# Two adaptive-norm blocks on one core: a new order at the end of the first layer, its last dense rows read from PSUM, and the second layer's first weights loaded and split inside it

## What is computed

```
mod = silu(c) @ wmod                       # per layer: sa, ca, ga, sb, cb, gb
# first layer
h = layernorm(x) * (1 + ca) + sa
x = x + ga * small_attention(h)
h = layernorm(x) * (1 + cb) + sb
p = softmax(h @ centroids.T / 0.1)         # 64 clusters
query_sel = any(p > 0.01, over clusters)   # per row
cluster_sel = any(p > 0.01, over all rows) # per cluster
dense = h @ weight.T + bias
x = x + gb * where(query_sel & cluster_sel[assignments], dense, 0)
# second layer
h = layernorm(x) * (1 + ca) + sa
q, k, v = h @ w_q, h @ w_k, h @ w_v        # 32 heads on 8 key heads, width 128
x = x + ga * causal_attention(q, k, v) @ w_o
h = layernorm(x) * (1 + cb) + sb
x = x + gb * (silu(h @ gate) * (h @ up)) @ down
```

## Time and profile before

| | us |
|---|---|
| median of 3 runs | 1952.21 (1950.08 to 1952.51) |
| the profiled execution | 1954.34 |
| its span, first to last instruction | 1952.6 |
| TensorE busy | 1858.4 (95%) |
| VectorE busy | 1229.1 (63%) |
| ScalarE busy | 1127.5 (58%) |
| GpSimd busy | 468.3 (24%) |

### The profile page before, as it was taken

The page is one execution under the profiler, slowest core; times in us unless marked ns, Lnnn a source line. Parts: engine busy times, 40 slices in busy tenths (PEclk is TensorE's granted clock), DMA queues, the critical chain, the costliest instruction groups (busy, mean ns, idle before and its releaser), DMA issues. The chain is left out here.

```text
span 1952.6 us, 30013 instructions
## 1 busy us (share of the span) xinstructions
PE 1858.4 (95%) x9227; PEld 1548.6 (79%) x9227; DVE 1229.1 (63%) x2962; ACT 1127.5 (58%) x2617; POOL 468.3 (24%) x474
## 2 busy tenths in 40 slices
PE   6897489999999999999999999999999979999999
PEld 4465378888888888888888888888888867788887
DVE  5577566766666666666666666667666676543534
ACT  5463466666666666666666666656666654433423
POOL 3121441414233231313423121240312052010010
PEclk8798699999999999999999999999999999999999
DMA  9100265565646545466654645455554475211010
GB/s 353 64 1 1 108 180 161 167 185 156 201 138 195 157 152 172 144 199 184 200 173 148 178 131 175 132 164 153 155 175 121 151 221 168 70 55 56 14 59 21
DMA packets 170381, 275.30 MB, mean 141 GB/s; under 512 B 18745, under 2 KB 111929, under 8 KB 170305
## 3 DMA queue, kind: packets, MB, share of 16 engines
q1 hardware_dynamic: 167760, 270.18, 44.9%
q10 hardware_dynamic: 2544, 4.19, 0.7%
HBM read 173.65 MB, written 100.66 MB: 140 GB/s over the span
## 5 line engine op out<-in xcount | busy, mean ns | idle before, releaser
L2018 DVE CUSTOM_DVE_ANT_0 ps<-ps,mask 128x512 f32<-128x512 f32 (+3 forms) x512 | 236.3, 524 | 339.7 <-PE ps L1573 339.7
L1534 PE MATMUL ps<-hA,wq 128*128 128x512 f32 x1536 | 386.0, 400 | 1.1 <-DVE qT L2003 0.8
L1606 PE MATMUL ps<-wo,oT 128*128 128x512 f32 x1536 | 372.1, 393 | 5.6 <-POOL wo L1392 5.6
L1842 ACT ACTIVATE pt<-pd 128x1280 fp32r<-128x1280 f32 x128 | 163.2, 1275 | 353.8 <-PE ps L1588 344.2
L1606 PEld LDWEIGHTS ps<-wo,oT 128*128 128x128 f32 x1536 | 286.7, 189 | 64.3 <-POOL wo L1392 5.8
L1534 PEld LDWEIGHTS ps<-hA,wq 128*128 128x128 f32 x1536 | 279.0, 188 | 57.9 <-issue 0.9
L1823 ACT ACTIVATE probs<-ps,nmax 128x512 f32<-128x512 f32 (+3 forms) x512 | 262.7, 532 | 47.4 <-DVE nmax L2018 47.3
L1831 ACT ACTIVATE probs<-probs,rinv 128x512 f32<-128x512 f32 (+3 forms) x512 | 246.2, 552 | 31.5 <-DVE rinv L2024 31.5
L1588 PE MATMUL ps<-pt,V 128*128 128x512 f32 (+2 forms) x1152 | 251.8, 348 | 8.1 <-DVE pt L2042 8.1
L1573 PE MATMUL ps<-kT,qT 128*128 128x512 f32 (+2 forms) x1152 | 224.9, 340 | 0.0
L1588 PEld LDWEIGHTS ps<-pt,V 128*128 128x128 f32 x1152 | 196.2, 189 | 34.7 <-issue 10.2
(11 more groups left out here) (214 smaller groups left out, 2554.9 us busy)
## 6 DMA issues: line engine op xcount, KB each, us to landing
turned_blocks<-tp SPq DMA_DIRECT2D x128, 640.0 KB, 2.9
pd<-turned_blocks SPq DMA_DIRECT2D x512, 160.0 KB, 3.3
wq_in<-in_L_attn_w_q_dram SPq DMA_DIRECT2D x16, 1024.0 KB, 6.4
wo_in<-in_L_attn_w_o_dram SPq DMA_DIRECT2D x16, 1024.0 KB, 7.0
wm<-in_L_wmod_dram SPq DMA_DIRECT2D x6, 2048.0 KB, 13.3
X<-in_L_attn_x_dram SPq DMA_DIRECT2D x4, 1024.0 KB, 11.2
wk_in<-in_L_attn_w_k_dram SPq DMA_DIRECT2D x16, 256.0 KB, 3.8
wv_in<-in_L_attn_w_v_dram SPq DMA_DIRECT2D x16, 256.0 KB, 4.1
```

Source lines behind the costliest of these rows:

```text
L1534: last = nc.tensor.matmul(ps[:, bank, :], w[i][:, c, cols], hT[k][:, c, b * S:(b + 1) * S], start=(c == 0 and n == 0), stop=(c == DC - 1 a ...
L1606: last = nc.tensor.matmul(ps[:, bank, :], oT[x_][:, b, h, r * P:(r + 1) * P], wo[y_][:, h, :], start=(h == 0 and n == 0), stop=(h == GQ - ...
L1842: nc.scalar.activation(flat(pt[0][:]), flat(pd[:, u % 2]), ACT.Copy).then_inc(phi_done, 1)
L2018: nc.vector.tensor_tensor_reduce(out=v, in0=v, in1=mask[:, TB * P - KEYS[i]:], scale=-1.0, scalar=3e38, op0=ALU.add, op1=ALU.min, accum_ou ...
```

## The change

- DVE: `with_dense` becomes two functions, `gate_dense` (L747) and `add_rows` (L751). The gate of sequence 0 stands before `add_outputs(2)`, its adds between the two halves of `add_outputs(3)`. cluster_hits(2), gate and adds of sequence 1 stand before the second layer's modulations; the gate of sequence 2 stands between `cluster_logits(3)` and `cluster_hits(3)`, its adds behind the threshold. Gate and adds of sequence 3 come after the first two sequences have been selected and their statistics taken. `inverse_2(0)` stands in the middle of select_rows(1), `inverse_2(1)` between gate and adds of sequence 3.
- The last sequence's dense tiles (12 to 15) aren't drained: the gate reads them from PSUM. Tiles 14 and 15 use the banks of the attention update (BANK_U), and `turn(3, ...)` uses banks 0 and 1 alone.
- PE: linear(14) stands before the transpose of the maximum.
- ACT: the four last drains are gone, `modulated_2(0)` stands before root_2(1), and modulated_2 waits for `mods_done`.
- SP: the load of the first Q weights goes to a tile over X's first tiles (`wq_next`). It is issued in the first block, once X's first four tiles are stored and normal_2(0) has read them, and the stores of tiles 4 to 15 are queued behind it.
- Pool: the first K and V weights are split in the first block, into memory over `dense`, once sequence 0 is selected. The prologue of the second block begins with the wait for the Q load and the first Q head.

The semaphore `w_hi` of the second block is renamed `w_high` and made earlier; this and its uses are left out below.

```diff
@@ -222,7 +222,13 @@
         l0 = ExitStack()
         with l0:
+            with ExitStack() as early:
+                wq_next = sb(early, "wq_next", [P, DC, D], F32)
             X = sb(l0, "X", [P, NT, D], F32)
+            with ExitStack() as early:
+                wk = [sb(early, f"wk{i}", [P, DC, HD], F32R) for i in range(2)]
+                wv = [sb(early, f"wv{i}", [P, DC, HD], F32R) for i in range(2)]
             with ExitStack() as early:
                 c_in = sb(early, "c_in", [B, 2, D], F32)
@@ -329,7 +337,11 @@
             def bank_of(k):
                 if k < DC:
                     return (0, 1, BANK_U, BANK_U + 1)[k]
-                return k % 2 + (BANK_U if k >= DC * (len(JOBS) - 2) else 0)
+                return k % 2
+            def bank_of_dense(t):
+                return BANK_D + t % 2 if t < NT - 2 else BANK_U + t % 2
             def tiles_of(b):
                 return slice(TB * b, TB * (b + 1))
@@ -372,6 +384,11 @@
                     for t in range(NT):
                         sp.wait_ge(x2_done, t + 1)
                         sp.dma_start(mid_t[t // TB][:, t % TB, :], X[:, t, :]).then_inc(mid_stored, 16)
+                        if t == TB - 1:
+                            sp.wait_ge(mid_stored, 16 * TB)
+                            sp.wait_ge(xh_2, 1)
+                            sp.dma_start(wq_next[:], w_q.rearrange("(c p) n -> p c n", p=P)[:, :, 0:D]).then_inc(q_in, 16)
                     sp.wait_ge(mid_stored, 16 * NT)
                     sp.wait_ge(kv_in, 32)
@@ -420,6 +437,15 @@
                             pool.wait_ge(taken, chunk(2, b, c) + 1)
                             nc.gpsimd.tensor_tensor(hP[b % 2][:, 1, c, :], hT2[:, c, :], hP[b % 2][:, 0, c, :].bitcast(F32),
                                                     ALU.subtract).then_inc(low2, 1)
+                    pool.wait_ge(x2_done, TB)
+                    pool.wait_ge(kv_in, 32)
+                    nc.gpsimd.tensor_copy(wk[0][:], wk_in[:]).then_inc(w_high, 1)
+                    pool.wait_ge(w_high, 1)
+                    nc.gpsimd.tensor_tensor(wk[1][:], wk_in[:], wk[0][:].bitcast(F32), ALU.subtract).then_inc(wk_split, 1)
+                    nc.gpsimd.tensor_copy(wv[0][:], wv_in[:]).then_inc(w_high, 1)
+                    pool.wait_ge(w_high, 2)
+                    nc.gpsimd.tensor_tensor(wv[1][:], wv_in[:], wv[0][:].bitcast(F32), ALU.subtract).then_inc(wv_split, 1)
                     for i in range(PAIR):
                         for c in range(DC):
                             pool.wait_ge(taken, chunk(3, i, c) + 1)
@@ -617,10 +643,7 @@
                     modulated2(3, range(2, DC))
                     drain(11)
                     copy_columns2(3)
-                    drain(12)
                     clusters(3)
-                    for t in range(TB * (B - 1) + 1, NT):
-                        drain(t)
                     def root_2(i):
                         act.wait_ge(var_2, i + 1)
@@ -634,6 +657,7 @@
                         last.then_inc(xh_2, 1)
                     def modulated_2(i):
+                        act.wait_ge(mods_done, 4)
                         for c in range(DC):
                             k = chunk(3, i, c)
                             act.wait_ge(turned, k + 1)
@@ -642,8 +666,8 @@
                     root_2(0)
                     normal_2(0)
+                    modulated_2(0)
                     root_2(1)
-                    modulated_2(0)
                     normal_2(1)
                     modulated_2(1)
@@ -713,8 +737,9 @@
                         by_tile = lambda k: red[:, k].rearrange("p (t e) -> p t e", t=TB)
                         nc.vector.tensor_tensor(o_t[:, :, 0:E0], by_tile(2), by_tile(1), ALU.mult).then_inc(o_done, 1)
-                    def add_outputs(b):
-                        for t in range(TB * b, TB * (b + 1)):
+                    def add_outputs(b, tiles=range(TB)):
+                        for r in tiles:
+                            t = TB * b + r
                             dve.wait_ge(upd_ps, t + 1)
                             nc.vector.tensor_tensor(X[:, t, :], X[:, t, :], ps[:, BANK_U + t % 2, :], ALU.add).then_inc(x1_done, 1)
@@ -739,14 +764,21 @@
                         link(nc.vector.tensor_scalar(qsel[:, tiles_of(b)], cred[:, 2], THRESHOLD, None, ALU.is_gt))
                         link(nc.vector.tensor_tensor(top[:], pr[:] if b == 0 else top[:], pr[:], ALU.max))
-                    def with_dense(b):
+                    def gate_dense(b):
                         dve.wait_ge(rows_sb, 2 * B)
                         for t in range(TB * b, TB * (b + 1)):
-                            dve.wait_ge(drained, t + 1)
-                            last = nc.vector.scalar_tensor_tensor(dense[:, t, :], dense[:, t, :], qsel[:, t:t + 1], gb_rows[:, b, :],
+                            if b < B - 1:
+                                dve.wait_ge(drained, t + 1)
+                                rows = dense[:, t, :]
+                            else:
+                                dve.wait_ge(dense_ps, t + 1)
+                                rows = ps[:, bank_of_dense(t), :]
+                            last = nc.vector.scalar_tensor_tensor(dense[:, t, :], rows, qsel[:, t:t + 1], gb_rows[:, b, :],
                                                                   ALU.mult, ALU.mult)
                         link(last)
+                    def add_rows(b):
                         for t in range(TB * b, TB * (b + 1)):
                             last = nc.vector.tensor_tensor(dense[:, t, :], dense[:, t, :], X[:, t, :], ALU.add)
                         link(last)
@@ -803,6 +835,7 @@
                     cluster_logits(0)
                     outputs(2)
                     cluster_hits(0)
+                    gate_dense(0)
                     add_outputs(2)
                     statistics2(2)
@@ -811,31 +844,34 @@
                     cluster_logits(1)
                     outputs(3)
                     cluster_hits(1)
-                    add_outputs(3)
+                    add_outputs(3, range(2))
+                    add_rows(0)
+                    add_outputs(3, range(2, TB))
                     statistics2(3)
                     cluster_logits(2)
                     normal2(3)
+                    cluster_hits(2)
+                    gate_dense(1)
+                    add_rows(1)
                     dve.wait_ge(mods_sb, len(MODS))
                     mods_finish(link, 1, MOD_SA, 6, tmp_g)
                     dve.sem_inc(mods_done, 1)
-                    cluster_hits(2)
-                    with_dense(0)
-                    with_dense(1)
                     cluster_logits(3)
-                    with_dense(2)
+                    gate_dense(2)
                     cluster_hits(3)
                     nc.vector.tensor_reduce(topc[:], top[:].rearrange("p t k -> p k t"), AX.X, ALU.max).then_inc(chosen, 1)
                     dve.wait_ge(chosen, TOP_TURNED)
                     link(nc.vector.tensor_reduce(topv[:, 0:1], ps[0:NCL, BANK_M, 0:P], AX.X, ALU.max))
                     link(nc.vector.tensor_scalar(topv[:, 1:2], topv[:, 0:1], THRESHOLD, None, ALU.is_gt))
                     nc.vector.tensor_scalar(selb[:], ones[:], topv[:, 1:2], None, ALU.mult).then_inc(chosen, 1)
-                    with_dense(3)
+                    add_rows(2)
                     dve.wait_ge(chosen, ROWS_SPREAD)
-                    def select_rows(b):
-                        for t in range(TB * b, TB * (b + 1)):
+                    def select_rows(b, tiles=range(TB)):
+                        for r in tiles:
+                            t = TB * b + r
                             nc.vector.copy_predicated(X[:, t, :], ps[:, BANK_P, :].bitcast(I32), dense[:, t, :]).then_inc(x2_done, 1)
-                        dve.wait_ge(x2_done, TB * (b + 1))
+                        dve.wait_ge(x2_done, t + 1)
                     def inverse_2(i):
                         v = tiles_of(i)
@@ -846,11 +882,14 @@
                     select_rows(0)
                     statistics(mv_2, 0, TB, var_2)
-                    select_rows(1)
+                    select_rows(1, range(2))
                     inverse_2(0)
+                    select_rows(1, range(2, TB))
                     statistics(mv_2, TB, 2 * TB, var_2)
+                    gate_dense(3)
+                    inverse_2(1)
+                    add_rows(3)
                     select_rows(2)
-                    inverse_2(1)
                     select_rows(3)
                     statistics(mv_2, 2 * TB, NT, var_2)
@@ -943,11 +982,13 @@
                     def linear(t):
                         b, r = t // TB, t % TB
-                        if t >= 2:
+                        if 2 <= t < NT - 2:
                             pe.wait_ge(drained, t - 1)
+                        if t >= NT - 2:
+                            pe.wait_ge(x1_done, NT)
                         if r == 0:
```

(17 more changed lines are left out.)

13 lines of the change are left out of this document (7 added, 6 removed).

## The result

The changed kernel took 1942.06 us, median of five runs (1936.46 to 1942.76), against 1952.21 for the kernel before beside it (also five runs, 1950.08 to 1958.59): ratio 0.9932, 95% interval 0.9914 to 0.9951. (The quotient of the two medians is 0.9948.) Its profiled execution took 1936.46 us, span 1934.7. In two later sessions, each beside fresh runs of the kernel before, the same program gave 1936.73 against 1956.03 (0.990, 0.9878 to 0.9921) and 1937.53 against 1954.41 (0.9921, 0.9906 to 0.9936). Over all four sessions the kernel before has a median of 1954.75 in 66 runs, over three of them the changed one 1937.99 in 17, with a standard deviation of 2.8 to 2.9 us each. The medians are 10.2, 19.3 and 16.9 us apart session by session, 16.8 when pooled. So the gain is about 17 us, and one median of five can be off by several.

The account below looks back on a forecast made before the run. TensorE, busy 95%, was the bound, so only its wait between first and second layer could give time: K 14.9 us earlier plus 0.4 at Q, 15.3 off 1952.2, gives 1936.9 us; range 1933.5 to 1942.5.

Parts of the forecast that it names:

- The first adds: In the first block, gate_dense(0) ahead of add_outputs(2) delays DVE by 0 to 1.3 us, taken as 0.3.
- The logits: cluster_logits(3) on DVE comes at 170.9 instead of 174.68, bound by TensorE's dots(3); gain 3.8 us, not 5.3.
- To the selection: From the logits to the first select_rows on DVE: reached at 181.0 against 197.68, 16.6 us earlier.
- The stretched tensor_scalar: Closing step of the first late statistics on DVE, lengthened beside Pool's splits by 0 to 1.3 us, taken as 0.9.
- DVE as the last engine: End of the first block: DVE, after waiting for root_2(1), ends at 213.8, 2.5 us after Pool.
- K and Q: Second block's start on TensorE: K at 214.2 instead of 229.06, 14.9 us earlier; Q's wait goes, 0.4 with overlap.
- The rest of the program: From the first Q projection to the end: distance unchanged within 1 us, so the 15.3 us gain arrives whole.
- B: Rival: no DVE and Pool collision on the path, dots(3) without the 0.3; gain 17.4, median 1934.8; chance 0.15.
- C: Rival: Pool and DVE collide everywhere, eight Pool operations up to 1.3 us each; gain 6.7, median 1945.5; chance 0.14.
- D: Rival: SP's stores behind the Q load go one after another and end at 226.7; 1950 us; chance 0.06.
- E: Rival: the second layer's loop over 16 groups gains a wait, at 1.5 us a group 1960.9 us; chance 0.04.

Follow-up runs that it names:

- gate_in_halves: Changed kernel with gate_dense(0) cut in two, tile 3's gate moved between the two halves of add_outputs(2); 1938.22 us, ratio 0.9912.
- weights_only: Kernel before with only the early Q weight load and the early K and V splits added; 1955.07 us, ratio 0.9992.
- splits_later: Changed kernel with Pool's four split operations behind inverse_2(0) instead of behind the selection of sequence 0; 1936.68 us, ratio 0.9904.
- order_only: Changed kernel without the early weights: Q loaded, K and V split in the second block as before; 1940.49 us, ratio 0.9916.
- drains_kept: Changed kernel with the last four dense tiles copied by ACT and gated from SBUF, as before; 1943.51 us, ratio 0.9943.
- root_first: Changed kernel with root_2(1) before modulated_2(0), inverse_2(1) before gate_dense(3), and select_rows(2) before add_rows(3); 1938.94 us, ratio 0.9916.

## Why the prediction was right, and where it was off

The forecast was 1936.9, a gain of 15.3 us. By distances from c2 the gain up to Q is 15.8 (14.9 to 17.0), by the pooled medians 16.8; the first median of five, 1942.06, is a gain of 10.2 and lay inside the range by only 0.4 us, which was luck; whether chance or the session made it high isn't shown. The traces show that the mechanism was right in every large term. Step by step:

- **The first adds.** The gate of tile 3 ahead of them cost 1.1 us; the prediction took 0.3 between 0 and 1.3. It saw that the second pair of adds hangs on the first, and then trusted DVE's idle 1.57 us all the same; and it had this gate at 0.7 us where it took 1.38 beside Pool. gate_in_halves shows that it was avoidable.
- **The logits.** Predicted at 170.9, which is 49.2 behind c2; measured 49.7. DVE waits 0.26 us for dots(3), so the bound is TensorE, as said. The miss is the 0.8 us of the step before, less 0.3 to 0.4 that was set aside for the way to DVE and wasn't needed. But it was close: DVE was to be ready 1.2 us ahead of the logits and was ready only 0.26 ahead, because gate_dense(1) and add_rows(1), beside Pool's subtractions, took 5.91 and 3.45 us instead of 2.8 and 2.5. With 0.3 us more DVE would have been the bound again. add_rows(0) was free: the adds behind it still waited 0.89 us.
- **To the selection.** 10.1 us predicted, 10.0 measured, and the whole step 16.2 us earlier where 16.6 stood.
- **The stretched tensor_scalar.** Taken as 0.9, measured 0.98 - 0.17 = 0.81; the small step of inverse_2(1) also 0.9 against 0.95 - 0.16 = 0.79. normal_2(0) 8.2 behind the select, measured 8.19. The prediction had weighed a rule of the Trainium skill (SBUF — State Buffer, Who interferes with whom) here: a DVE operation with two inputs in SBUF, or a tensor_scalar that uses both ports, and a GpSimd operation that reads SBUF wait for each other's whole instruction. The traces agree: the step is 0.98 us where the splits stand beside it (weights_only too) and 0.17 where they don't (splits_later, order_only), and a gate batch with both tensors in SBUF was stretched (3.75 us, drains_kept) where one with one of them in PSUM wasn't (2.73).
- **DVE as the last engine.** Predicted end 32.8 behind the select with Pool 2.5 us earlier, measured 32.60 and 30.24; K at 33.2, measured 32.93. The wait for root_2(1) was 2.89 us (predicted some 2), and root_first shows that it lay on the path: moving the root gave 2.4 us.
- **K and Q.** Q was to follow K 5.0 us later without a wait: 4.42 in the first trace, 5.25 in the two others, by how much of K ran at the lower clock. No wait in any.
- **The rest of the program.** "Whole" was wrong as a statement on one trace and right on the average. Q to end is 1718.1, 1720.8 and 1719.1 in the three traces with the old order, and 1716.0 to 1726.5 in the others. It was to be the same within 1 us; it differs by 2.6 between two traces of the kernel before and by 6.7 between three of the changed one. The prediction had no term for this.

Of the rivals, B fell because the stretches happened. C was half right: DVE was stretched in more places than the two counted, by 0.7 us at the gate of tile 3, which was on the path, and by some 4 at gate and adds of sequence 1 (in before the first gate batch lost 2 in that place), which TensorE's own work hid; behind the logits it stayed at the two small steps. D and E did not occur: the last store was issued 5 us before the block's end, and the second layer's mean from Q to the end is 1719.3 for the three traces with the old order and 1719.9 for the three of the changed kernel.

## What to carry to other kernels

Walk back from the first late matmul to the engine that releases it, and move off that chain whatever can be done in another engine's or its own idle time: here 13.5 of 15 us came from a new order of the work around a decision that all rows wait for, and 1 to 2 from loading and splitting weights early. After each such move ask which engine now ends the stretch, and look at its waits again: three small moves more took 3 us off the changed kernel's path, though the medians of its runs don't show them. When two kernels differ by less than a per cent, compare distances between the same two events in several traces, from a point ahead of the change; in the three traces of the changed kernel the one from c2 to K repeated to 0.01 us, while medians of five and six of its runs moved by 5. It isn't free of the clock either: in the two traces of the kernel before it differs by 1.3.

## What the runs showed of the hardware

- TensorE reaches c2 after 116.4 to 123.2 us in fourteen traces whose TensorE work up to there is the same, with a granted clock of 0.50 to 1.00 between 90 and 100 us (0.99 or 1.00 in the four earliest, 116.4 to 117.0; 0.50 in the four latest, 121.7 to 123.2; 0.80 to 0.94 in the six between). That is 7 us in 1940, more than most single edits here are worth.
- After an idle time the first matmuls of a stretch may run at either level: linear(14) took 5.15 us after 10.4 us of idling (granted clock 0.53) and 2.91 after 3.4 (1.00); K took 4.54 to 5.46 us in fourteen traces, after 3.2 to 7.6 us of idling.
- A DVE step of 0.17 us took 0.98 or 0.99 us beside a Pool split in eight traces with the early splits, and 0.17 in the six where the splits stand later. A gate batch with one tensor in PSUM ran 2.73 us beside Pool's subtractions, with both in SBUF 3.75, and Pool's four went from 5.27 to 6.35.
